# A fourth padded buffer for the q, k and v tiles of a two-layer vision kernel

## What is computed

```python
x = x + _L0_conv_ref(_gn(x), ...)
x = x + _L1_conv_ref(_gn(x), ...)
```

```python
qkv = einsum('bchw,oc->bohw', x, w_qkv) + b_qkv
qkv = depthwise_conv3x3(qkv, w_dw) + b_dw          # zero padding of 1
q, k, v = split(qkv, 3, axis=1)                    # each (b, heads, 48, n)
q = l2norm(q, axis=2); k = l2norm(k, axis=2)       # over the 48 channels
attn = softmax(einsum('bhdn,bhdm->bhnm', q, k) * temperature)
out = einsum('bhnm,bhdm->bhdn', attn, v)
out = einsum('bchw,oc->bohw', out, w_proj) + b_proj
```

## Time and profile before

| | |
|---|---|
| time, median of 3 runs | 15378.18 us (15376.93 to 15384.7) |
| time of the profiled execution | 15378.3 us |
| its span, first to last instruction | 15376.4 us |
| mean granted TensorE clock | 0.962 of full speed |
| mean HBM traffic | 94 GB/s |

### The profile page before, as it was taken

The page is one execution under the profiler, slowest core; times in us unless marked ns, Lnnn a source line. Parts: engine busy times, 40 slices in busy tenths (PEclk is TensorE's granted clock), DMA queues, the critical chain, the costliest instruction groups (busy, mean ns, idle before and its releaser), DMA issues.

```text
span 15376.4 us, 245780 instructions
## 1 busy us (share of the span) xinstructions
PE 13151.0 (86%) x60888; PEld 7921.7 (52%) x60888; DVE 12874.0 (84%) x13813; ACT 11085.9 (72%) x22746; POOL 10505.7 (68%) x4158
## 2 busy tenths in 40 slices
PE   6888888888888898888988889888898888988889
PEld 4555455554555545555455554555445554455544
DVE  8999669996799867998579985899848998499984
ACT  5887578875788657886578866788667886678865
POOL 5998069980699707997079960899608995099950
PEclk9999999999999999999999999999999999999999
DMA  3333023430234203342033420334203342033420
GB/s 110 127 127 114 20 92 128 134 98 20 96 128 137 91 20 101 128 137 87 20 109 127 135 82 20 115 128 135 75 20 120 128 135 71 20 129 126 132 66 25
DMA packets 907782, 1465.69 MB, mean 95 GB/s; under 512 B 38912, under 2 KB 891904, under 8 KB 893664
## 3 DMA queue, kind: packets, MB, share of 16 engines
q1 hardware_dynamic: 906560, 1452.37, 29.6%
HBM read 1350.07 MB, written 102.17 MB: 94 GB/s over the span
## 4 chain that ended last, share of the span: by engine, by line
PE 42%; DVE 20%; issue 20%; POOL 9%; ACT 6%; DMA 2%; DVEq 1%; ACTq 1%; POOLq 0%; SPq 0%
DVE area L1018 12%; PE ps L659 9%; PE ps L843 9%; PE ps L854 8%; POOL area L1495 7%; DVE area L1036 6%; PE ps L646 3%; PE ps L637 2%; PE ps L625 2%; ACT ps L1299 2%; POOL area L1505 2%; DMA area<-bc_rows 1%; PE ps L589 1%; PE ps L734 1%; ACT area L1268 1%
## 5 line engine op out<-in xcount | busy, mean ns | idle before, releaser
L1018 DVE TENSOR_TENSOR_SCAN area<-ps,hst,area 128x384 f32<-128x384 f32 x9216 | 8593.7, 997 | 221.3 <-ACT ps L1299 191.2
L1495 POOL TENSOR_TENSOR area<-area 128x1152 f32<-128x1152 f32 x3072 | 8001.6, 2640 | 46.0 <-POOL area L1484 28.1
L1299 ACT ACTIVATE ps<-area,a_neg 128x384 f32<-128x384 f32 x9216 | 5306.9, 581 | 1579.3 <-DVE area L1018 1379.0
L659 PE MATMUL ps<-area,ident 128*128 128x384 f32 x12672 | 4674.6, 502 | 173.3 <-ACT area L1284 129.3
L659 PEld LDWEIGHTS ps<-area,ident 128*128 128x128 f32 x12672 | 2322.4, 196 | 1861.9 <-ACT area L1284 399.1
L646 PE MATMUL ps<-ident,area 128*128 128x128 f32 x17280 | 2464.9, 280 | 5.2 <-ACT area L1268 5.2
L1479 POOL TENSOR_TENSOR area<-area,ones 128x2304 f32<-128x2304 f32 x8 | 43.3, 5414 | 3506.7 <-ACT area L1224 3386.8
L1438 ACT ACTIVATE area<-ps,t_neg,area 128x768 f32<-128x768 f32 x1728 | 1617.7, 986 | 964.8 <-PE ps L843 964.8
L646 PEld LDWEIGHTS ps<-ident,area 128*128 128x128 f32 x17280 | 2234.6, 196 | 59.2 <-ACT area L1268 9.5
L1505 POOL TENSOR_TENSOR area<-area 128x1152 f32<-128x1152 f32 x768 | 2026.9, 2639 | 129.5 <-ACT hst L1244 129.0
L637 PE MATMUL ps<-ident,area 128*128 128x128 f32 x8640 | 1481.4, 281 | 496.8 <-ACT area L1268 433.7
(11 more groups left out here) (128 smaller groups left out, 9823.3 us busy)
## 6 DMA issues: line engine op xcount, KB each, us to landing
area<-bc_rows SPq DMA_DIRECT2D x1536, 768.0 KB, 6.5
xz<-x_normed SPq DMA_DIRECT2D x144, 288.0 KB, 4.7
area<-in_x SPq DMA_DIRECT2D x18, 1728.0 KB, 10.1
area<-x_padded SPq DMA_DIRECT2D x24, 1250.0 KB, 5.6
z_raw<-z_st SPq DMA_DIRECT2D x144, 192.0 KB, 4.5
area<-z_raw SPq DMA_DIRECT2D x8, 3456.0 KB, 12.9
x_padded<-x_st SPq DMA_DIRECT2D x120, 200.0 KB, 7.3
x_normed<-area SPq DMA_DIRECT2D x9, 1728.0 KB, 7.9
```

The lines of the kernel that those rows point to most:

```text
L659: m = e.matmul(ps[:, 5 + j, 0:CH], ident[:], hb[:, i % NH, j], start=i == 0, stop=i == N - 1)
L1018: e.tensor_tensor_scan(rev(hb[:, i % NH, j], k), rev(ps[:, 2 + j, 0:CH], k), rev(dbu[:, i % NH, j], k), hst[:, i, j:j + 1], ALU.mult, ALU. ...
L1299: e.activation(ps[:, 2 + j, 0:CH], dlt[:, par, j], ACT.Exp, scale=a_neg[:, j, k, i:i + 1]).then_inc(da, 1)
L1495: e.tensor_tensor(dbu[:, i % NH], du[:, par], row_b[:, q % 2, i % ROWS:i % ROWS + 1].broadcast_to([128, J, CH]), ALU.mult).then_inc(dbus, 1)
```

## The change

A fourth padded buffer is made of memory that lies idle in this stage (the second of the two padded buffers that the first layer's convolution uses). A table says which tile goes to which buffer. Tiles 0 to 3 have one each, tile 4 takes tile 0's and tile 5 takes tile 1's. PE and ScalarE project tile 3 right behind tile 2, ahead of the transposes of v, then tile 4 behind the transposes, and tile 5 behind the q norms. ScalarE waits for a convolution only from tile 4 on, and for that of tile i - 4. POOL clears four borders, as its loop runs over `xp2`.

```diff
+PAD_OF = (0, 1, 2, 3, 0, 1)
...
-        xp2 = [ar(XP2 + i * PADS, PAD).rearrange("p (h w) -> p h w", h=HP) for i in range(3)]
+        xp2 = [ar(XP2 + i * PADS, PAD).rearrange("p (h w) -> p h w", h=HP) for i in range(3)] + xpads[1:]
...
-            conv_taps(e, b * 108, i, cv2, xp2[i % 3], (v_v[:, p], q_v[:, p], kz[:, p])[kind], w_dw, b_dw)
+            conv_taps(e, b * 108, i, cv2, xp2[PAD_OF[i]], (v_v[:, p], q_v[:, p], kz[:, p])[kind], w_dw, b_dw)
...
                         for i in range(3):
                             qkv(i)
+                        qkv(3)
                         wait_cv2(e, b, 0)
                         for g in range(5):
                             transpose_v(0, g)
-                        qkv(3)
+                        qkv(4)
                         for c in range(NC):
                             q_norm(0, c)
-                        qkv(4)
                         qkv(5)
                         k_norms(0)
...
-                    if i >= 3:
-                        wait_cv2(e, b, i - 3)
+                    if i > 3:
+                        wait_cv2(e, b, i - 4)
...
-                            e.activation(xp2[i % 3][:, ds(cc * 16 + (8 * s + 1), 8), 1:1 + W],
+                            e.activation(xp2[PAD_OF[i]][:, ds(cc * 16 + (8 * s + 1), 8), 1:1 + W],
...
                         for i in range(3):
                             pad_qkv(i)
+                        pad_qkv(3)
                         for g in range(5):
                             copy_vt(e, b, 0, g)
-                        pad_qkv(3)
+                        pad_qkv(4)
                         wait_cv2(e, b, 1)
                         e.activation(sqq[0], q_v[:, 0], ACT.Square).then_inc(qsq, 1)
                         for c in range(NC):
                             q_norm(0, c)
-                        pad_qkv(4)
                         pad_qkv(5)
                         k_norms(0)
```

## The result

| | before | changed |
|---|---|---|
| median of 20 runs | 15380.92 us (15372.58 to 15384.7) | 15356.42 us (15354.31 to 15361.22) |
| profiled execution | 15378.3 us | 15360.3 us |
| ratio | | 0.9985, 95% interval 0.9978 to 0.9992 |

The change is 24.5 us faster, 3.1 us an image. The two profiled executions are 17.9 us apart: that of before lies low in its runs, that of the changed kernel high.

A forecast was written before the change was run, and what follows sets the result against it. No engine is full; VectorE paces from tile 0's convolution, then idles 7.96 us before the Newton steps. Six images lose 0.02 us, two lose 2.0 and win 1.68: 0.8 us slower, 15379 us, range 15355 to 15393.

The forecast's parts named there:

- The wait for the buffer: Ahead of the first pair's k norms, tile 5's projection waits until convolution 2 frees its buffer; forecast to vanish.
- the idle time before the Newton step: VectorE waiting for ScalarE's roots of the k norms; 53.6 us over eight images, forecast some 50 us.
- Nothing won: First pair, six images: k norms at half clock end 7.74 us behind the square, against 7.72 us today.
- the 2.0 us charged for the second group of scores: First pair, two images: scores starting 1.68 us earlier would have a slow second group, losing 2.0 us.
- The transposes: Transposes of v, behind tile 3's projection: its last chunk ready 0.3 us before convolution 0 ends; cost nothing.
- POOL's memsets: Four memsets for a fourth border, below 0.4 us, free with 15 us of cover before convolution 0.
- a microsecond won ahead of them is won in the span: Time won before PE and ScalarE exchange first-pair scores and exponentials was claimed to shorten the whole span equally.
- the sum that ends at the first pair's scores: Over eight images, 6 x 0.02 + 2 x (2.0 - 1.68) = 0.8 us slower; forecast chance 0.62.
- rival B: First pair's k norms start at half clock, which rises while they run: 5.46 us; 21 us won, 15357 us; chance 0.15.
- A: First pair's k norms keep full clock or regain it at once: 4.08 us; 32.0 us less, 15346 us; chance 0.08.
- C: First pair's second group of scores slow in all eight images: about 13 us slower, 15391 us; chance 0.12.

## Why the prediction was wrong

**The first pair of heads: right, nearly to the number.** The wait for the buffer is gone, the k norms start 0.06 us behind the square, they run at half clock, in 7.84 us (7.68 forecast), and the idle time before the Newton step is 51.5 us (some 50 forecast). "Nothing won" in most images holds, and so do the 2.0 us charged for the second group of scores in two images (1.96 us, in the third and fifth). The transposes weren't held up, and POOL's memsets cost nothing that shows.

**The step that failed: "a microsecond won ahead of them is won in the span", and with it the sum that ends at the first pair's scores.** I carried everything behind them along unchanged. It isn't: the second pair's k norms, some 180 us later, took 7.68 us in seven of eight images and take 4.57 us now. I had those 7.68 us in rows 10 and 11, used them as a price, and never asked what they would do themselves if they met the clock a few tenths of a microsecond off: in the kernel before, the fall of the clock lay 0.03 to 0.11 us short of where, in these traces, the fast k norms begin (2.91 to 2.83 against 2.94 us). I had also opened only five images there; one of the other three showed 4.56 us, in the kernel before. That term, -2.72 us, and the -0.33 us net of the two rows behind it make 3.05 us, more than the 2.7 us by which the mean image became shorter. The first pair gives back 0.23 us of it net (-0.26 us up to the end of its k norms, +0.49 us in its exponentials), and stages that the table doesn't list give back the small rest.

**How a near-zero sum became 24.5 us.** The run with 0.2 us added shows that the shift alone does it: 15356.4 us. The runs with added work show that an edit of some tenths to 1.4 us doesn't move the length of an image by its own size: the changed kernel's own 0.3 us at the first pair came out as 2.7 us an image, 1.4 us of work as 0.2 us, 0.47 us as 2.4 us. The lengths keep to a series. From first pad to first pad, 84 of the 91 image lengths in the thirteen traces lie within 0.3 us of 1891.0, 1894.4, 1897.8, 1901.2, 1904.6, 1908.0 or 1911.4 us, values 3.4 us apart. What holds an image to them is not shown. That an image's length settles where its work meets the changes of PE's clock in the same way each time fits the runs: with filling at the first pair alone all images are 1901.2 or 1901.3 us long from square to square, and in all eight the clock falls 2.80 to 2.87 us ahead of the second pair's k norms. But that is argued, and no run tests it.

**The rivals.** The time is that of rival B (15357 us), but not by its mechanism: the clock never rose during the first pair's k norms. It rose so at the second pair, 0.14 to 0.38 us behind their start in all eight images, where I had named rows 11 as the case against it; the price of B was a sum for another place, and that it met the time is luck. A is refuted in the change and built in the run with the seven matmuls: 4.18 us, 3.66 us won in each image. Of these 29 us against the change 1.5 us were left, since the second pair gave the rest back. C happened in two images of eight. The Trainium skill's sentence, "activity releases the throttle" ("TensorE: Matmul & The Clock Gate", Part 1, "What's actually happening"), agrees with the filling matmuls of 384 columns in so far as the clock stayed up behind them (4.18 us for the k norms, 7.84 us without), and not with the k norms themselves, whose 36 matmuls of 2 columns ran 7.8 us on end at 0.50.

The measured time lies in the range (15356 in 15355 to 15393), but that is luck too, since rival B had set its lower end. The forecast itself, 0.8 us slower, had the wrong sign: I looked for a gain at the first pair alone.

## What to carry to other kernels

Where PE runs at half clock behind its idle gaps, price an edit against every later stretch that runs at half clock, not only against the one it touches: a shift of 0.2 us was worth 24 us here. Before crediting an edit of a few tenths of a per cent to its idea, run the old kernel with a small delay in the same place. And fill PE's gaps with matmuls whose result nobody reads: 18 of them an image won 72 us on top of the change, three times what the buffer had won.

## What the runs showed of the hardware that I had not expected

- The time is not monotonic in the work: on the kernel before, 0.47 us more on VectorE an image cost 16 us, 1.4 us cost 3 us, and 0.2 us on ScalarE won 24 us.
- Here the small matmuls of the k norms neither brought the clock back nor kept it up: 36 of 128x2 took 7.84 us, at a granted 0.50 from 1646.1 to 1653.9, though PE was busy all the while; and at the second pair the clock fell from 1.00 to 0.50 while they ran, behind 3.30 us in which PE was busy for 3.30 us (1832.3 to 1835.6).
- The same stretch of work, 0.1 us off against the clock, took 4.57 or 7.68 us (72 images, table above).
- PE idle for 1.52 us was followed by half clock in one image and by full clock in another (5.42 us for the four chunks, in the run with 1.4 us more on VectorE, against 7.12 us in rows 4): the length of the gap alone doesn't tell.
